# A four-layer residual kernel: two low parts swapped, two stores per tile, products regrouped in the last tiles, identity transposes in the opening

## Time and profile before

| what | before |
|---|---|
| median of three runs | 639.48 us |
| the profiled execution, its own time | 641.35 us |
| its span, first to last instruction | 639.6 us |
| mean granted TensorE clock | 0.997 |
| busy: TensorE | 624.6 us (98%) |
| busy: VectorE | 334.6 us (52%) |
| busy: ScalarE | 174.6 us (27%) |
| busy: GpSimd | 63.7 us (10%) |

### The profile page before, as it was taken

How to read it: one execution, slowest core, us unless ns; L and a number is a source line. 1 busy time by engine, 2 the same in 40 slices (tenths; PEclk the granted TensorE clock), 3 DMA queues, 4 the chain that set the end, 5 groups by cost and what they waited for, 6 DMA issues and landing times.

```text
span 639.6 us, 9237 instructions
## 1 busy us (share of the span) xinstructions
PE 624.6 (98%) x3472; PEld 601.9 (94%) x3472; DVE 334.6 (52%) x615; ACT 174.6 (27%) x315; POOL 63.7 (10%) x143
## 2 busy tenths in 40 slices
PE   6999999979999999999999999999999999999996
PEld 4999999879999999999999889999999999999996
DVE  2488998998989629000012295444434444333432
ACT  3344234254242136111122353111111111111111
POOL 3101010031003000000000041111111111111100
PEclk9999999998999999999999999999999999999999
DMA  9932420380000031100002101111111111110001
GB/s 264 259 115 61 134 71 1 41 257 15 1 2 1 1 34 17 26 1 0 0 0 66 34 13 55 67 66 66 66 66 66 66 66 66 66 66 33 34 34 66
DMA packets 55374, 37.67 MB, mean 59 GB/s; under 512 B 26412, under 2 KB 50988, under 8 KB 55348
## 3 DMA queue, kind: packets, MB, share of 16 engines
q1 hardware_dynamic: 55348, 37.31, 20.5%
HBM read 28.91 MB, written 8.39 MB: 58 GB/s over the span
## 4 chain that ended last, share of the span: by engine, by line
PE 95%; DMA 1%; DVE 1%; issue 1%; SPq 0%; ACT 0%; POOL 0%; ACTq 0%; DVEq 0%
PE acc L1069 51%; PE acc L1202 33%; PE acc L1190 4%; PE aux L1057 2%; PE acc L1244 1%; PE acc L1245 1%; DMA g<-in_L_cond_W_dram 1%; PE aux L1128 1%; PE acc L1057 1%; PE aux L1236 0%; DVE a_lo L765 0%; POOL g L422 0%; DVE bst L767 0%; DVE hg_lo L754 0%; DVE w_lo L747 0%
## 5 line engine op out<-in xcount | busy, mean ns | idle before, releaser
L1202 PE MATMUL acc<-h_hi,xt_hi 128*128 128x408 f32 x384 | 98.2, 357 | 0.0
L1202 PE MATMUL acc<-h_lo,xt_hi 128*128 128x408 f32 x384 | 94.7, 348 | 0.0
L1202 PE MATMUL acc<-h_hi,xt_lo 128*128 128x408 f32 x384 | 94.6, 347 | 0.0
L1069 PE MATMUL acc<-hg_hi,w_hi 128*128 128x352 f32 (+2 forms) x384 | 88.0, 338 | 3.8 <-issue 3.7
L1069 PE MATMUL acc<-hg_hi,w_lo 128*128 128x352 f32 (+2 forms) x384 | 86.8, 335 | 0.0
L1069 PE MATMUL acc<-hg_lo,w_hi 128*128 128x352 f32 (+2 forms) x384 | 86.7, 334 | 0.0
L1069 PEld LDWEIGHTS acc<-hg_hi,w_hi 128*128 128x128 f32 x384 | 67.2, 190 | 5.5 <-issue 4.4
L1202 PEld LDWEIGHTS acc<-h_hi,xt_lo 128*128 128x128 f32 x384 | 71.5, 188 | 0.2
L1202 PEld LDWEIGHTS acc<-h_lo,xt_hi 128*128 128x128 f32 x384 | 71.5, 188 | 0.1
L1202 PEld LDWEIGHTS acc<-h_hi,xt_hi 128*128 128x128 f32 x384 | 67.3, 189 | 1.4
L1069 PEld LDWEIGHTS acc<-hg_hi,w_lo 128*128 128x128 f32 x384 | 68.5, 191 | 0.0
(11 more groups left out here) (176 smaller groups left out, 726.2 us busy)
## 6 DMA issues: line engine op xcount, KB each, us to landing
x_st<-in_x_dram SPq DMA_DIRECT2D x64, 128.0 KB, 2.8
out_dram<-out_sb SPq DMA_DIRECT2D x16, 512.0 KB, 2.6
g<-in_L_cond_W_dram SPq DMA_DIRECT2D x8, 512.0 KB, 7.1
w_st<-in_L_cond_W_dram SPq DMA_DIRECT2D x8, 512.0 KB, 4.9
a_t<-in_L_cond_weight_dram SPq DMA_DIRECT2D x8, 512.0 KB, 6.0
w_raw<-in_L_cond_weight_dram SPq DMA_DIRECT2D x8, 512.0 KB, 4.3
a_raw<-in_L_cond_lora_A_dram SPq DMA_DIRECT2D x5, 128.0 KB, 3.4
a_raw<-in_L_cond_lora_A_dram SPq DMA_DIRECT2D x20, 32.0 KB, 1.9
```

The source lines that it names most:

```text
L1069: last = pe.matmul(acc[0:a.shape[-1], slot, bank * BANK:bank * BANK + c1 - c0], a[:, k, :], b[:, k, c0:c1], start=(at == 0 and n == 0), st ...
L1202: last = pe.matmul(acc[:, slot, bank * BANK:bank * BANK + PART], a[:, slot, k, :], b[:, k, c0:c0 + PART], start=(k == 0 and n == 0), stop= ...
```

## The change

- Opening: 14 transposes of the identity (WARM) into an unused PSUM place before `turn_w3(0)`, and 16 more (BRIDGE) behind it. SyncE loads W2's first slice before A3 and Wr. The A3 and Wr transposes are split: k tiles 0 to 5 (A3's six, then Wr's six) before the first products, k tiles 6 and 7 in k step 1. Two of three banks of k step 0 are multiplied before `turn_w3(1)`, the third behind it. ScalarE's and VectorE's copies follow.
- VectorE and ScalarE between pass 8 and pass 9: `w1_high(0)` and `w1_low(0)` come before W0's parts; of `quantise(4, 1)`, the threshold 3 goes behind `w0_low(1)` and threshold 4 behind `w0_low(3)`; `split_b2` is earlier, and `quantise(3, 1)` goes ahead of `w2_low(7)`.
- Output: `o_done` is signalled for each bank; a copy waits for its own bank alone; each tile is stored by two DMAs, the columns of banks 0 and 1, then those of bank 2.
- Last tile: bank 0 of its k = 6 and 7 products moves behind the bank 1 products of k = 3 and k = 4 in the closing step.

```diff
+        WARM, BRIDGE = 14, 16
         def a3_at(bank, k0, k1):
-            return acc[:, 0, bank * BANK:...]
+            return acc[:, min(bank, 1), 2 * BANK:...]
 # SyncE
                 if k == 0:
+                    load_w2(0)
                     sp.dma_start(a3_st, ...)
                     sp.dma_start(wr_st, Wr)
-                    load_w2(0)
...
                     for bank in range(2):
                         sp.wait_ge(o_act[bank], t + 1)
+                    c = BANK_2[h]
+                    sp.dma_start(out_rows[..., 0:c], out_sb[:, h, 0:c]).then_inc(out_done[h], 16)
                     sp.wait_ge(o_dve, t + 1)
-                    sp.dma_start(out_rows[...], out_sb[:, h]).then_inc(out_done[h], 16)
+                    sp.dma_start(out_rows[..., c:D], out_sb[:, h, c:D]).then_inc(out_done[h], 16)
 # ScalarE
-            for k in range(3):
-                w0_high(k)
             w1_high(0)
-            for k in range(3, 6):
+            for k in range(6):
                 w0_high(k)
...
-                    act.wait_ge(o_done, t)
                     for bank, (where, c0, c1) in enumerate(...[:2]):
+                        act.wait_ge(o_done, t * 3 + (bank - 2))
                         act.copy(out_sb[:, 1 - h, c0:c1], where)
 # VectorE
             add_delta(0)
+            split_b2()
             quantise(0, 0)
             quantise(0, 1)
             w2_low(3)
-            split_b2()
...
             quantise(3, 0)
+            quantise(3, 1)
             w2_low(7)
-            quantise(3, 1)
...
             quantise(4, 0)
-            quantise(4, 1)
             add_bp(...)
-            for k in range(3):
-                w0_low(k)
             w1_low(0)
-            for k in range(3, KT):
+            w0_low(0)
+            w0_low(1)
+            quantise(4, 1, (3,))
+            w0_low(2)
+            w0_low(3)
+            quantise(4, 1, (4,))
+            for k in range(HALF, KT):
                 w0_low(k)
             w1_low(1)
 # TensorE
             pe.wait_ge(made, 2)
+            for _ in range(WARM):
+                turn_tile(acc[:, 0, 2 * BANK:2 * BANK + P], ident[:])
             turn_w3(0)
+            for _ in range(BRIDGE):
+                turn_tile(acc[:, 0, 2 * BANK:2 * BANK + P], ident[:])
             pe.wait_ge(a3_in, 32)
+            turn_a3((0, 1))
+            pe.wait_ge(w_split, 1)
+            tile_of(0, 0, 0, 0, three_pairs(0, 0), (0, 1))
             for k in range(KT):
+                if k == 1:
+                    pe.wait_ge(a3_done, 2)
+                    turn_a3((2,))
                 if k + 1 < KT:
                     turn_w3(k + 1)
...
-                tile_of(0, k, k, 0, three_pairs(0, 0))
+                tile_of(0, k, k, 0, three_pairs(0, 0), (0, 1, 2) if k else (2,))
...
-                        last = products(k, h, ... (0, 2))
+                        last = products(k, h, ... (0, 2) if k < KT - 2 else (2,))
                     else:
                         products(k, s, (1,))
+                        if k in (3, 4):
+                            products(k + 3, s, (0,))
...
                         for where, c0, c1 in in_banks(s, s, 0, D):
-                            done = three(where, ...)
-                        done.then_inc(o_done, 1)
+                            three(where, ...).then_inc(o_done, 1)
```

More of the change, by code:

```diff
@@ L395, in _ @@
                 load_x(t, t * P)
+            BANK_2 = [list(in_banks(h, h, 0, D))[2][1] for h in range(2)]
             def tile_io(t, h, load, store):
@@ L534, in _ @@
                     w2_high(0)
-                    act.wait_ge(a3_t, 1)
-                    for bank, (k0, k1) in enumerate(a3_tiles):
+                if k in (0, 1):
+                    act.wait_ge(a3_t, k + 1)
+                    for bank in ((0, 1), (2,))[k]:
+                        k0, k1 = a3_tiles[bank]
                         act.copy(hg_hi[:, k0:k1, C_H:C_LOW2], a3_at(bank, k0, k1)).then_inc(a3_hd, 1)
@@ L831, in split_b2, with quantise @@
                                          op0=ALU.mult, op1=ALU.subtract).then_inc(b2_done, 1)
-            def quantise(x, part):
+            def quantise(x, part, steps_=None):
                 n = a_t[:, x, 0:D].rearrange("p (k i) -> p k i", k=KT)
@@ L838, in quantise @@
                     link(dve.tensor_scalar(q[:], n, th(0), steps[:, 0:1], ALU.is_gt, ALU.mult))
-                for j in ((1, 2), (3, 4), (5, 6))[part]:
+                for j in steps_ or ((1, 2), (3, 4), (5, 6))[part]:
                     link(dve.tensor_scalar(qtmp[:], n, th(j), steps[:, j:j + 1], ALU.is_gt, ALU.mult))
@@ L1060, in _, with tile_of @@
             WIDTHS = (C_LOW2, C_A, C_ALL)
-            def tile_of(stage, k, at, slot, pairs):
+            def tile_of(stage, k, at, slot, pairs, banks=(0, 1, 2)):
                 pe.wait_ge(h_ready, table_count(stage, k))
@@ L1067, in tile_of @@
                 for n, (a, b) in enumerate(pairs):
-                    for bank, (c0, c1) in enumerate(thirds(WIDTHS[stage])):
+                    for bank in banks:
+                        c0, c1 = thirds(WIDTHS[stage])[bank]
                         last = pe.matmul(acc[0:a.shape[-1], slot, bank * BANK:bank * BANK + c1 - c0],
@@ L1071, in tile_of @@
                                          stop=(at == KT - 1 and n == len(pairs) - 1), skip_group_check=True)
-                last.then_inc(h_used if at < KT - 1 else acc_done, 1)
+                if 2 in banks:
+                    last.then_inc(h_used if at < KT - 1 else acc_done, 1)
             def three_pairs(stage, h):
@@ L1091, in _, with turn_a3 @@
             pe.wait_ge(made, 2)
+            for _ in range(WARM):
+                turn_tile(acc[:, 0, 2 * BANK:2 * BANK + P], ident[:])
             turn_w3(0)
-            pe.wait_ge(a3_in, 32)
[L1094 to L1099, removed]
+            def turn_a3(tiles):
+                for c0, c1, st in ((0, ER, a3_st), (ER, NR, wr_st)):
+                    for bank in tiles:
+                        k0, k1 = a3_tiles[bank]
+                        for k in range(k0, k1):
+                            last = turn_tile(a3_at(bank, k0, k1)[:, k - k0, c0:c1], st[:, k * P:(k + 1) * P])
+                last.then_inc(a3_t, 1)
+            for _ in range(BRIDGE):
+                turn_tile(acc[:, 0, 2 * BANK:2 * BANK + P], ident[:])
+            pe.wait_ge(a3_in, 32)
+            turn_a3((0, 1))
+            pe.wait_ge(w_split, 1)
+            tile_of(0, 0, 0, 0, three_pairs(0, 0), (0, 1))
             for k in range(KT):
+                if k == 1:
+                    pe.wait_ge(a3_done, 2)
+                    turn_a3((2,))
                 if k + 1 < KT:
@@ L1224, in tile @@
                     if ahead is not None:
-                        last = products(k, h, (0,) if not finish else (0, 1, 2) if ahead else (0, 2))
+                        last = products(k, h, (0,) if not finish else (0, 1, 2) if ahead else (0, 2) if k < KT - 2 else (2,))
                     else:
                         products(k, s, (1,))
+                        if k in (3, 4):
+                            products(k + 3, s, (0,))
                     if finish and k == 0:
@@ L1255, in tile @@
                         for where, c0, c1 in in_banks(s, s, 0, D):
-                            done = three(where, (hgt_h[:], hgt_l[:]), (b3_hi[:, c0:c1], b3_lo[:, c0:c1]),
-                                         stop=True)
-                        done.then_inc(o_done, 1)
+                            three(where, (hgt_h[:], hgt_l[:]), (b3_hi[:, c0:c1], b3_lo[:, c0:c1]),
+                                  stop=True).then_inc(o_done, 1)
                     if ahead is not None and k == KT - 1:
```

22 lines of the change are left out of this document (12 added, 10 removed).

## The result

The kernel after takes 633.64 us (median of 4 runs, 633.60 to 633.69 us), the kernel before 639.57 us in the same comparison (4 runs, 639.43 to 640.11 us). The ratio is 0.9907, with a 95% interval of 0.9891 to 0.9922: 5.9 us less, against a forecast of 6.6 us less (632.9 us, range 631.2 to 637.2 us).

What follows compares the result with a forecast made beforehand. TensorE, busy 98% of the span, was taken to bound the kernel. Opening 3.4, middle 2.3 and end 0.9 us sum to 6.6 us, so 639.5 us becomes 632.9 us, range 631.2 to 637.2 us.

Steps and rivals of the forecast that it cites:

- The forecast case: Whole kernel: gains in opening, middle and end, with the clock rising early in the opening; 632.9 us, chance 0.60.
- The opening: Start of the kernel: identity transposes bring the fast clock earlier; 3.4 us won, bounds 2.4 and 4.3 us.
- the working: Step-by-step estimate of times; in the opening, fast clock from 9.4 us and k step 1 starting at 15.9 us.
- Each rise comes 4.3 us after a restart: TensorE's clock, opening and pass 9: it rises 4.3 us after unbroken work restarts, read from two stretches.
- The rival by the rule of the Trainium skill: Opening: transposes do not raise the clock, so it loses 0.2 us; 636.5 us in all, chance 0.28.
- The middle: Pass 8 to 11: the gain is what VectorE wins, 2.3 us and not 5.4 us; bounds 1.5 and 3.1 us.
- The waits forecast: Middle: TensorE would wait 1.3 us before delta(6), and shortly before turn_w1(2) and delta(7).
- gives back what it gets: Middle: late W0 rows cost VectorE its 2.1 us, and the clock stays low; 638.8 us, chance 0.08.
- never waited for them: Middle: argument against late W0 rows, that VectorE had not waited for these rows in the kernel before.
- The end: Last tile and store: regrouping wins 0.4 us and stores 0.5 us, 0.9 us together; bounds 0.4 and 1.4 us.
- The rival with a cost in every tile: Expert product of each tile: signals by bank delay TensorE; at 0.6 us a tile 642.5 us, chance 0.04.
- The parts add: Sum: opening, middle and end gains add to 6.6 us, as VectorE's opening chain moves with TensorE's k = 7.

Runs made afterwards that it cites:

- before again: The kernel before, unchanged, run and profiled a second time: 639.8 us, ratio 0.9999; its profiled execution took 639.60 us.
- end alone: Only the signals by bank, two stores and regrouped last-tile products, on the kernel before: 638.69 us, ratio 0.9981.
- opening alone: Only WARM, BRIDGE, the new order of W2 and A3 and two banks early, on the kernel before: 638.12 us, ratio 0.9972.
- regrouped products alone: Only the last tile's bank 0 products regrouped, on the kernel before, without signals by bank or two stores: 639.51 us, ratio 0.9993.
- middle alone: Only the new order on VectorE and ScalarE, on the kernel before: 637.44 us, ratio 0.9958.
- after again: The kernel after, unchanged, run again in a later group: 633.25 us, ratio 0.9900.
- after without its three waits: Kernel after with delta 6 one k step later, W1's row tile 2 transposes later, w1_low(3) behind threshold 5 of quantise(5): 631.74 us, ratio 0.9865.

## Why the prediction was right

**The kind and the size.** The forecast case, all three parts with the clock rising in the opening, is what happened: 5.9 us measured, 6.6 us forecast; the later comparison with the kernel after unchanged gives 0.9900, 6.5 us (639.73 and 633.25 us by the medians). The profiles, by the starts of pass 8's first transpose and of stage 3's first product (us), show where each version stands:

| kernel | pass 8's transposes | from there to stage 3 |
|---|---|---|
| before, before again | 131.6, 129.8 | 241.1, 241.1 |
| end alone | 130.0 | 241.1 |
| opening alone | 127.5 | 241.0 |
| regrouped products alone (longer low clock) | 129.2 | 242.5 |
| middle alone | 129.3 | 238.6 |
| middle and end, opening of before | 130.4 | 238.7 |
| after, after again | 127.3, 126.8 | 238.8, 238.9 |
| after without identity transposes | 129.9 | 238.7 |
| after with WARM alone | 129.0 | 240.0 |
| after without its three waits | 129.4 | 235.8 |

**The opening: right in its mechanism, 3.4 us where 2.5 to 2.9 us are to be had.** The step that was mis-sized is the first: the opening of before, taken from one execution. The prediction noted that this execution was 1.9 us above the median and then took its savings, on the assumption that the excess lay elsewhere and stayed. It lay just there: the step at 18.9 us was the latest of six. In that one pair of profiles the opening moved everything by 4.3 us, the upper bound. The opening of after, in turn, was 0.9 us better than the working had it: the clock was up at 6.6 us (5.0 us in the profile of after again), not 9.4 us, so WARM counted (I had let the 4.3 us start anew at 5.1 us); A3 landed at 8.7 us rather than 9.3 us; W3's row 1 got its identity by 10.7 us, not 12.4 us. Two errors offset one another in part, the stretch of before priced some 1.7 us too long and that of after 0.9 us too long; that the sum came out so near is in part luck. "Each rise comes 4.3 us after a restart" was a pattern of two cases in one execution and is not a constant: the second profile of before has the rise some 2 us after 14.20 us.

**The rival by the rule of the Trainium skill falls.** The page "TensorE: Matmul & The Clock Gate" of the Trainium skill (Part 4: PE-mode transpose) says that transposes do not count as busy. This case's traces do not agree: in the profiles after and of the version with WARM alone, the clock rose when TensorE had done nothing but transposes (recorded as MATMUL on `ident`), and taking out the 30 of the identity costs 2.5 us. What lay between the two readings in the rows of before was right to be left open at 0.60 to 0.28: they showed transposes with waits between them, and no unbroken run.

**The middle: right in mechanism and size**, 2.3 us forecast, 2.4 us alone and 2.35 us in the first pair of profiles; five profiles with the new order and no late row of W0 have 2.2 to 2.5 us. `w1_low(1)` started at 145.85 us; without the opening's 4.27 us that is 150.1 us, 2.2 us before 152.30 us, where the working had 2.1 us (VectorE's idle 1.81 us and 0.3 us of `split_b2`). The waits forecast, 1.3 us, short, short, were 1.3, 0.7 and 0.5 us. The whole stall (3.7 us) plus the low clock behind it (1.6 to 1.8 us) would have been 5.4 us, and the version that takes away all three waits shows what the difference was: with VectorE asked later, the same stretch is 5.3 us shorter than in before. The rival "gives back what it gets" did not come in the two profiles of after, where VectorE was never idle by over 0.1 us in front of W0's low parts. But it was near: one of them started as its high part was written, and with WARM alone a late row made VectorE idle for 1.47 us and left 1.1 us of the middle's gain. The prediction's "never waited for them" had given this too little weight.

**The end: right, 1.1 to 1.2 us for 0.9 us.** The regrouping measured 0.51 us for 0.4 us, the stores 0.6 us for 0.5 us (half of it an earlier issue, half a shorter time from issue to the end of the span), and their sum is inside its bounds. The rival with a cost in every tile has no trace in two tiles' window.

**The sum.** Alone, the parts gave 1.8 + 2.4 + 1.2 = 5.4 us, together 5.9 to 6.5 us. "The parts add" is roughly right; the opening alone gives less where five of six of its runs spend longer at the low clock. Why the low stretch behind the stall is longer in some executions stays open.

## What to carry to other kernels

When the time of the profiled execution lies well above the median of the runs, find the excess before summing savings on its rows, or profile a second execution: here it lay in the very stretch that was priced. When a stall of the busiest engine is removed, its gain is not the stall but what the engine that caused it wins; add up that engine's idle time between here and the next places where it is waited for. And filler work that raises the clock was worth under 1 us here until more of it spanned the next wait. Last, when an engine gets its work sooner, look at what feeds it: here the loads behind it were left without slack, and one late row cost half of the gain.

## What the runs showed of the hardware that I had not expected

- TensorE's clock rises on transposes alone: 14 identity transposes from 1.58 us, and the next eight, real ones, take 1.09 us (WARM alone) in place of 1.94 us (no identity transposes).
- It falls again soon: idle times of 1.97 and 1.65 us before A3's transposes were followed by a granted clock of 0.50, from 8.8 to 15.6 us and from 11.2 to 14.6 us; idle times of 0.22 to 0.41 us there were not, in four profiles. The same page of the Trainium skill ("Why this matters for your kernels") warns only of longer gaps than these; by that neither would have mattered. Here pass 8's transposes started 1.7 to 2.6 us later than in the profiles of after. In the middle of the kernel, waits of 1.3 to 1.6 us left the clock at 1.00 in every profile.
- The moment of the rise differs between executions of the same kernel, near 16.2 us and at 18.9 us in two profiles of before, and with it the time by 1.7 us.
- The granted clock of the record says 1.00 from the start of the opening, also while the pace is that of 1.2 GHz (5 to 14 us in before); so do the means of the runs. The pace of eight equal transposes (1.94 or 1.03 us) is the measure there.
